# Windowed channel attention with a depthwise convolution: the 128 partitions hold two halves of one image instead of two images

## What is computed

```
xn  = groupnorm(x, 32 groups)                      # two channels to a group, mean and variance over the image
qkv = depthwise3x3(w_qkv @ xn + b_qkv) + b_dw      # 1x1 product to 192 channels, then a 3x3 per channel, zero padding
q, k, v = windows of 8 x 8 pixels, 4 heads of 16 channels
attn = softmax(q k^T * temperature)                # channels x channels (16 x 16) in each window and head
out  = (attn v) * gelu(v w_mlp^T + b_mlp)          # the gate is exact gelu over the 64 pixels of a window
y    = x + w_proj @ out + b_proj
```

## Time and profile before

| | us |
|---|---|
| Median of three runs | 672.14 |
| The profiled execution | 675.23 |
| Its span in the trace | 673.4 |
| PE busy (share of the span) | 623.8 (93%) |
| PE weight loads busy | 547.5 (81%) |
| DVE busy | 504.5 (75%) |
| ACT busy | 481.4 (71%) |
| Mean granted TensorE clock | 0.982 |

### The profile page before, as it was taken

One profiled execution on the slowest core, in us unless ns is written; L12 is line 12 of the kernel. 1 busy time (PEld: TensorE's weight loads), 2 busy tenths in 40 slices (PEclk: granted clock), 3 DMA queues, 4 the chain that ended last, 5 costly groups with the idle time before them and its releaser, 6 DMA issues.

```text
span 673.4 us, 32951 instructions
## 1 busy us (share of the span) xinstructions
PE 623.8 (93%) x15300; PEld 547.5 (81%) x15300; DVE 504.5 (75%) x791; ACT 481.4 (71%) x631; POOL 0.3 (0%) x5
## 2 busy tenths in 40 slices
PE   3888799999999999999999999999999999999975
PEld 2787688888979888888879888898989888898963
DVE  4872588787988788786877678687867778687774
ACT  2642768687777878687787878787787868777743
POOL 0000000000000000000000000000000000000000
PEclk9898899999999999999999999999999999999996
DMA  8872114417071524314060412305050412303023
GB/s 363 267 220 73 34 35 144 150 42 253 22 247 50 183 98 118 113 44 153 4 195 6 135 67 73 130 8 195 4 180 24 136 67 70 127 4 127 4 82 49
DMA packets 29242, 72.32 MB, mean 107 GB/s; under 512 B 9801, under 2 KB 16329, under 8 KB 24233
## 3 DMA queue, kind: packets, MB, share of 16 engines
q1 hardware_dynamic: 28674, 68.57, 31.5%
q10 hardware_dynamic: 432, 1.65, 0.6%
HBM read 53.44 MB, written 16.78 MB: 104 GB/s over the span
## 4 chain that ended last, share of the span: by engine, by line
PE 87%; ACT 5%; DVE 3%; issue 3%; DMA 1%; ACTq 0%; DVEq 0%
PE unit_ps L750 28%; PE unit_ps L715 26%; PE rest_ps L867 10%; PE rest_ps L818 6%; PE rest_ps L844 5%; PE rest_ps L790 5%; PE rest_ps L828 4%; ACT z L337 2%; DMA patches<-in_hot 1%; PE rest_ps L684 1%; ACT dw L337 1%; PE rest_ps L715 1%; PE unit_ps L677 0%; DVE gate L521 0%; DVE scores L531 0%
## 5 line engine op out<-in xcount | busy, mean ns | idle before, releaser
L337 ACT ACTIVATE z<-unit_ps 100x768 f32<-100x768 f32 x244 | 184.7, 808 | 58.3 <-PE unit_ps L715 58.3
L715 PE MATMUL unit_ps<-consts,patches 64*100 64x192 f32 x1984 | 193.7, 335 | 8.6 <-ACT z L337 6.5
L750 PE MATMUL unit_ps<-z,dw 103*64 103x64 f32 (+2 forms) x6144 | 194.3, 224 | 3.2 <-issue 1.9
L750 PEld LDWEIGHTS unit_ps<-z,dw 103*64 103x64 f32 (+2 forms) x6144 | 185.7, 139 | 10.7 <-issue 8.6
L715 PEld LDWEIGHTS unit_ps<-consts,patches 64*100 64x100 f32 x1984 | 152.5, 163 | 25.6 <-ACT z L337 11.1
L337 ACT ACTIVATE qkv<-unit_ps 128x1024 f32<-128x1024 f32 x78 | 79.1, 1014 | 31.7 <-PE unit_ps L750 31.6
L867 PE MATMUL rest_ps<-gate,consts 128*128 128x256 f32 x256 | 74.7, 416 | 3.4 <-DVE gate L521 3.2
L531 DVE TENSOR_TENSOR scores<-rest_ps,consts 128x512 f32<-128x512 f32 x60 | 41.3, 689 | 48.7 <-PE rest_ps L790 48.6
L521 DVE TENSOR_TENSOR gate<-rest_ps,gate 128x512 f32<-128x512 f32 x64 | 44.1, 688 | 44.9 <-PE rest_ps L844 40.7
L358 ACT ACTIVATE v_t<-rest_ps 128x512 f32<-128x512 f32 x64 | 38.2, 596 | 40.9 <-PE rest_ps L828 39.4
L352 ACT ACTIVATE scores<-scores 128x512 f32<-128x512 f32 (+1 forms) x64 | 39.5, 617 | 29.1 <-DVE scores L538 27.5
(11 more groups left out here) (61 smaller groups left out, 533.5 us busy)
## 6 DMA issues: line engine op xcount, KB each, us to landing
staged<-in_x SPq DMA_DIRECT2D x17, 1024.0 KB, 4.9
out_y<-staged SPq DMA_DIRECT2D x15, 1024.0 KB, 5.4
T<-in_x SPq DMA_DIRECT2D x12, 1152.0 KB, 7.0
seen<-in_x SPq DMA_DIRECT2D x32, 256.0 KB, 3.1
qkv<-in_x SPq DMA_DIRECT2D x6, 1024.0 KB, 14.0
T<-in_x SPq DMA_DIRECT2D x3, 1088.0 KB, 6.8
staged<-in_x SPq DMA_DIRECT2D x2, 512.0 KB, 23.2
out_y<-staged SPq DMA_DIRECT2D x4, 256.0 KB, 3.1
```

What stands on the lines that cost most here:

```text
L337: return nc.scalar.activation(to, of, ACT.Copy)
L715: last = nc.tensor.matmul(to[0:NPATCH, t, b * QKV:(b + 1) * QKV], patches[image, b, g], w1[image], start=True, stop=True)
L750: last = nc.tensor.matmul(to[h * HW:(h + 1) * HW, m // 8, m % 8 * NW:(m % 8 + 1) * NW], dw[0:used, c, :], z[0:used, c, :], start=True, sto ...
```

## The change

The partitions become channel c of the upper half (rows 0 to 63) and channel c of the lower half (rows 64 to 127) of one image. A chunk is then one band of 16 rows of each half; an image has four bands, and four images make 16 chunks again. With that:

- Every DMA between the image and the partitions becomes two, one to or from partitions 0 to 63 and one to or from 64 to 127. T takes its neighbour rows from across the middle of the image; the first one comes by a small DMA (`halo_in`).
- The first load is one image (4 MB in 10 DMAs) instead of two. It fits into `qkv`'s space, so `prefill` of chunks 0 and 1 no longer waits for the statistics.
- The group product averages over four partitions instead of two. The mean and variance are made four times instead of twice, three of them inside the run, at chunks 3, 7 and 11.
- 48 slices instead of 32 go through `look`: two to a step in the first eight steps, then one to a step up to step 39.
- The border rows are loaded once. Three rows more take the top rows back where all rows are used, since top and bottom now meet in different halves: K goes from 109 to 112, and `top_rows` goes.
- `idle_products(24)` becomes `idle_products(4)`.
- ACT's queue loads the taps and the build table beside the image as before; those lines stay.

The diff, cut to its core:

```diff
-PAIRS = B // 2
+SIDE = H // 2
-BANDS = H // BAND
-CHUNKS = PAIRS * BANDS
+BANDS = SIDE // BAND
+CHUNKS = B * BANDS
-EDGES = 9
+EDGES = 12
-STATS = H // STAT_ROWS
+STATS = SIDE // STAT_ROWS
-LOOKS = (2, 2, 1, 1)
...
-    return n if n < BANDS else CHUNKS - 1 - n
+    return n % BANDS if n // BANDS % 2 == 0 else BANDS - 1 - n % BANDS
...
-    if (n, a) == (BANDS - 1, 0):
-        fill += [("mean", 1)]
-    if (n, a) == (BANDS - 1, 1):
-        fill += [("var", 1)]
+    if a == 0:
+        fill += [("mean", image) for image in next_image(n)]
+    if a == 1:
+        fill += [("var", image) for image in next_image(n)]
     return fill
+
+
+def next_image(n):
+
+    return [n // BANDS + 1] if n % BANDS == BANDS - 1 and n + 1 < CHUNKS else []
...
-    return min(i // BATCHES * sum(LOOKS) + sum(LOOKS[:i % BATCHES]), STATS)
+    early = 2 * BATCHES
+    return min(2 * i if i < early else STATS + i - early, (B - 1) * STATS)
...
-        first = [loaded[:, n * BAND:(n + 1) * BAND] for n in range(6)] + [staged[:, n] for n in range(2)]
+        first = [loaded[:, n * BAND:(n + 1) * BAND] for n in range(BANDS)]
...
+        sides = [slice(t * C, (t + 1) * C) for t in range(2)]
...
             def load_t(n):
                 sp.wait_ge(patches_ready, n)
-                lo, hi, to = band_rows(n)
-                sp.dma_start(T[:, to:to + hi - lo, 1:1 + W], halves[n // BANDS, :, lo:hi, :]).then_inc(t_in, 16)
+                for t in range(2):
+                    lo, hi, to = halo_rows(n, t)
+                    sp.dma_start(T[sides[t], to:to + hi - lo, 1:1 + W], x[n // BANDS, :, lo:hi, :]).then_inc(t_in, 16)
...
-                if n < 2:
-                    sp.wait_ge(seen_done, 2 * BANDS)
-                else:
-                    sp.wait_ge(stored[n % 2], (n // 2) * 16)
...
+                if n >= 2:
+                    sp.wait_ge(stored[n % 2], (n // 2) * 32)
+                for t in range(2):
+                    sp.dma_start(staged[sides[t], n % 2],
+                                 x[n // BANDS, :, chunk_rows(n, t), :]).then_inc(staged_in[n % 2], 16)
...
-            def top_rows(which, p):
-                wait_full(sp, ("dw", which * BANDS, 5))
...
+            def load_first(n, rows, done):
+                for t in range(2):
+                    top = t * SIDE + n * BAND
+                    sp.dma_start(first[n][sides[t], rows],
+                                 x[0, :, top + rows.start:top + rows.stop, :]).then_inc(done, 16)
...
+            sp.dma_start(T[sides[1], 0, 1:1 + W], x[0, :, SIDE - 1, :]).then_inc(halo_in, 16)
+            sp.wait_ge(x_last, 32)
+            sp.dma_start(z[NPATCH:K].rearrange("p c w -> p (c w)"), edges).then_inc(edges_in, 16)
...
                 if band == 0:
-                    pad(T[:, 0:1, :], pair)
+                    pad(T[sides[0], 0:1, :], pair, sides[0])
...
-                nc.vector.bn_stats(stats[:, p], seen[:, p % 2]).then_inc(seen_done, 1)
+                nc.vector.bn_stats(stats[:, p % STATS], seen[:, p % 2]).then_inc(seen_done, 1)
...
-            idle_products(24)
+            idle_products(4)
...
-                                           -bottom, bottom and left, bottom and right)
+                                           -bottom, bottom and left, bottom and right,
+                                           top, -(top and left), -(top and right))
...
-    group = (0.5 * (chan[:, None] // 2 == chan[None, :] // 2)).astype(f)
+    group = (0.25 * (chan[:, None] % C // 2 == chan[None, :] % C // 2)).astype(f)
```

More of the change, by code:

```diff
@@ L212, in build @@
         number = units()
-        halves = x.rearrange("(j b) c h w -> j (b c) h w", j=PAIRS)
-        bands = out.rearrange("(j b) c h w -> j (b c) h w", j=PAIRS)
         def wait_full(engine, unit):
@@ L272, in prefill @@
-                rows = slice(band_of(n) * BAND, (band_of(n) + 1) * BAND)
-                sp.dma_start(staged[:, n % 2], halves[n // BANDS, :, rows, :]).then_inc(staged_in[n % 2], 16)
-            def load_seen(i):
-                for p in range(looks_until(i), looks_until(i + 1)):
-                    if p >= 2:
-                        sp.wait_ge(seen_done, 2 * BANDS + p - 1)
-                    rows = slice(p * STAT_ROWS, (p + 1) * STAT_ROWS)
-                    sp.dma_start(seen[:, p % 2], halves[1, :, rows, :]).then_inc(seen_in[p % 2], 16)
@@ L404, in _ @@
                     v_up(i)
-                if (n, a) == (BANDS - 1, 2):
-                    deviation(1)
+                if a == 2:
+                    for image in next_image(n):
+                        deviation(image)
                 now = gelus_in(i)
@@ L472, in normaliser, with pad @@
                 link(nc.vector.tensor_tensor(norm[:, pair, 1:2], small[:, 4:5], small[:, 5:6], ALU.mult))
-            def pad(edge, pair):
+            def pad(edge, pair, rows=slice(0, P)):
                 size = edge.shape[1] * edge.shape[2]
-                over = zeros[:, 0:size] if size <= 2 * (BAND + 2) else zeros[:, 0:1].to_broadcast([P, size])
+                over = zeros[rows, 0:size] if size <= 2 * (BAND + 2) else zeros[rows, 0:1].to_broadcast(
+                    [rows.stop - rows.start, size])
                 over = over.rearrange("p (r c) -> p r c", r=edge.shape[1])
-                link(nc.vector.tensor_scalar(edge, over, norm[:, pair, 0:1], None, ALU.add))
+                link(nc.vector.tensor_scalar(edge, over, norm[rows, pair, 0:1], None, ALU.add))
             def pads(n):
@@ L639, in _ @@
                     look(p)
-                if looks_until(i) < STATS <= looks_until(i + 1):
-                    aggregate(1)
+                if a == BATCHES - 1:
+                    for image in next_image(n + 1):
+                        aggregate(image)
             scores_up(TAIL)
@@ L743, in depthwise @@
                 if v == 0:
-                    pe.wait_ge(edges_in, 16 * (1 + PIECES * sum(n >= m for m in (BANDS - 1, CHUNKS - 1))))
+                    pe.wait_ge(edges_in, 16)
                 used = rows_used(n)
```

86 lines of the change are left out of this document (46 added, 40 removed).

## The result

The changed kernel takes 692.96 us (median of 4, 685.65 to 695.64) beside 671.67 of the kernel before in the same comparison: ratio 1.0284, 95% interval 1.0191 to 1.0377, so about 20 us slower. The forecast was 674.6, its range ended at 681.5. The profiled execution took 695.64, the longest of the four; its span is 693.8. Times are medians and ratios are of means, which leave out the executions that took over 1.5% more than the kernel's shortest (two of e11_warm24, one of e8_t_halves_only).

The account below looks back on a forecast made before the run. The prediction took PE, 87% of the chain, to bound the kernel. Head -2.0, steady part +4.1 and tail +0.4 gave +2.5: 677.7 us against the profiled execution, 674.6 against the median, range 667 to 681.5.

Parts of the forecast that it names:

- Head, by the build: Head up to the first channel product: build table lands at 15.7, first channel product at 35.8 instead of 37.83; -2.0 us.
- rival 1: All transfers: both halves together reach the full 419 GB/s; head -6.3, total 670.3, or 667 without PE's stop; chance 0.23.
- Head, behind the image: Head after the image: T of chunk 1 lands at 47.7 to 50.4, costing PE 0 us at 230 GB/s.
- Rival 2: Depthwise units: PE's instructions come late behind slower half transfers; two more stops cost +6.8, giving 681.4; chance 0.17.
- rival 3: First channel products: with 20 fewer warming products PE starts cold at 1.2 GHz, costing 1.5 to 3 us; chance 0.08.
- Steady part: Steady chunks: two more image changes cost +2.8 and slices in third batches +1.3; together +4.1 us.
- Tail: End of the run: each last store becomes two, one more DMA issue on the path; +0.4 us (bounds 0 and 1).

Follow-up runs that it names:

- e11_warm24: The changed kernel with 24 warming products ahead of the statistics, as before, instead of 4: 681.59 us, ratio 1.0119.
- e8_t_halves_only: The changed kernel with partitions ordered 2c + t and single 128-partition transfers for all but T, which stays in halves; nothing left out: 678.46 us, ratio 1.0077.
- e1_joined: The changed kernel with each pair of 64-partition transfers made one over 128 partitions; output not the reference's: 671.58 us, ratio 0.9996.
- e7_t_first: The changed kernel with T of chunk 1 issued ahead of the second staged block, not behind it: 687.86 us, ratio 1.0213.
- e13_short20: The changed kernel with 20 more products, of one column each, ahead of the statistics: 679.48 us, ratio 1.0145.
- e14_long_same_count: The changed kernel with 9 products of 512 columns ahead of the statistics and 1 behind, replacing 4 and 6 of 192: 694.38 us, ratio 1.0308.
- e17_before_warm4: The kernel before with 4 warming products ahead of the statistics instead of 24, all transfers over 128 partitions: 672.03 us, ratio 1.0016.
- e5_no_change: e1_joined without the work of the image changes, all images normalised with image 0's numbers; output not the reference's: 662.95 us, ratio 0.9845.
- e4_two_queues: The changed kernel with upper halves' transfers on SP's queue and lower halves' on POOL's, each with its own semaphores: 686.15 us, ratio 1.0218.
- e15_joined_short20: e1_joined with 20 more products of one column ahead of the statistics: 675.91 us, ratio 1.0045.

## Why the prediction was wrong

1. **Head, by the build (-2.0).** The number held (-2.05), the way to it did not, so that is luck. The table was to land at 15.7 and set the head; it landed at 12.00, so the image beside it gave way, not the table. The weights were ready at 24.65, nearly as before, and the mean product waited for the image: the statistics were done at 29.87, where the sum had 27.5. The mean product came 1.8 us earlier than in the sum (29.93 for 31.7), and from there to the first channel product it took 1.8 us longer (5.85 for 4.08), most of it at the lower clock. The rate chosen, 230 GB/s, is near the 271 and 234 of the first two windows of 8.2 us; which of two transfers it would hold up was wrong. At 420 GB/s e1_joined shows -7.08, for which rival 1 had -6.3. (At 250 GB/s, an estimate in the prediction, the same steps give a sum of +1.7, where it has +1.9.)
2. **Head, behind the image (0).** This step failed. T of chunk 1 was to land between 47.7 and 50.4; it was there at 53.00. The image was in at 27.86, not 25.2, and the transfers behind it took 25.1 us, where the sum had 22.5 to 25.2. PE's hold was put at 0, and at 2.5 at most; the stop was 2.61. Moved ahead of one staged block (e7_t_first), T came in time and PE's stop behind DVE went, but one of 2.58 us without a releaser stood in its place, so T's lateness alone is not shown to cost the 2.61.
3. **Rival 2, late instructions (0.17).** This was the case, and the sum had it at nothing: the step that failed by most. Its mark, waits named "issue" in the depthwise units, is there: 3.48 us at 62.22, with no packet of instructions beside 1.16 MB of T. The argument against it was that steady chunks move 132 GB/s and show no such stop. That holds for the program and the transfers of before, not for others: there are three such stops, in turn 5, step 17 and step 29, and the trace of e13_short20, with 40 more records, has none of them. The changed kernel and e1_joined run the same 15,268 records of PE in the same order, so their starts can be set side by side. Of the 8.4 us that the middle stage of the changed kernel is longer, some 6 come at five places where PE's instructions are late (1.8, 0.5, 0.9, 1.3 and 1.8 us at 128.79, 137.24, 206.37, 255.32 and 372.79), and 1.3 between 84.1 and 90.8, where the granted clock is 0.50. The rule of the Trainium skill, "Runtime: NRT & Kernel Launch", section "Instruction fetch mechanics", that the queue mostly hides the fetch, holds for most places in every kernel here; it failed once by 1.91 us in the kernel before, and by 3.48, 1.58, 0.96, 1.51 and 1.75 us here.
4. **The step that was missing.** "The head has 20 products less" was weighed as a cold start (rival 3) and, under rival 1, as a chance to lose a stop. That it could also bring stops was not. Given half transfers, the same kernel takes 692.96, 686.50 or 679.48 us with 0, 10 or 20 small products more (their intervals touch; those of the changed kernel and of e11_warm24 do not). With 128 partitions it makes no difference in the steady part.
5. **Rival 3, a cold start (0.08).** Not the cause of the 20 us: e14_long_same_count is busy nearly as long ahead of the mean product as e11_warm24 (7.99 us, 9.75) and no faster than the changed kernel, and e17_before_warm4 loses nothing. But it was there, since PE waited for the statistics: 1.3 us ahead of the first channel product (2.61 for 1.35), where rival 3 had 1.5 to 3. The lower clock cost more behind the long stops: 2.6 us in the first depthwise units and 1.3 in the channel unit after them.
6. **Steady part (+4.1).** Right for the work that it names: e1_joined takes 4.3 us more than before in the middle stage, and a change is worth 1.5 where 1.40 were taken. Plain chunks without a stop still repeat after 38.0. The changed kernel lost 12.76 there; the rest is point 3.
7. **Tail (+0.4).** 2.8, and 1.5 in e1_joined. PE has a stop of 1.75 us at 675.58, as in e1_joined (2.31 at 650.34), named "issue" in both, that before doesn't have there. It too belongs to the place of the instructions: e5_no_change lacks it.

Of the 24.3 us between the spans of the changed kernel and e1_joined, 5.0 are the image's, 9.5 those of points 2 and 3 before the first scores, 8.4 come in the middle stage, 1.3 in the tail. The first comes with the halves alone, 1.3 of it by the clock; the rest needs the halves and the place of the instructions together, since either without the other lacks most of it (e1_joined; e13_short20, whose span is 6.6 us longer than e1_joined's, all of it in its first channel product, 6.72 later).

Why a fetch beside a half transfer stops PE at one place and not at another, the traces answer in part. PE's instructions come in packets of 16 KB by queue q8, 120 packets for the 30,834 instructions of PE in the trace, so one for every 256 or so:

```profile
q8 instruction: 120, 1.97, 1.2%
```

Counted by 256 from PE's first instruction, the stops without a releaser lie at the same place in each block, the 194th or 195th, in all twenty traces. That goes for every one of over 0.65 us behind 38 us, but for the 1.4 us ahead of one channel unit, which all kernels have, and one of 0.88 in e4_two_queues. The packet for the next block starts when PE has entered the one before it, 0.60 us later in the median of the kernel before and 0.95 in the changed kernel. At the stops at 62.22, 128.79, 255.32 and 372.79 it started 6.20, 4.90, 4.96 and 5.56 us later, behind data of q1, and PE went on 1.4 to 1.5 us after it had ended. A delay of 6.40 us from 431.71 on stopped nothing, since PE had work for 9.0 us in that block; depthwise records use one up in 3.8 (128 of the 192 in 5.75). So a stop takes a long transfer under way as PE enters a block (in the steady part only kernels with half transfers show such stops), and quick work in that block. Products added upstream move the work against the blocks, and a later start moves both against the transfers. Open is in which order the DMA engines serve the two queues, how much of the delay comes from T's small packets, and why executions of one kernel differ by 10 us.

## What to carry to other kernels

Splitting one transfer of 128 partitions into two of 64 takes a third off the rate here, and a second queue does not give it back: choose the layout by the stride that lets one transfer reach all partitions (half t of channel c at partition 2c + t did, at 64t + c didn't). A slower bulk transfer can be paid twice, by who waits for its data and by TensorE's instructions behind it; the second price moves with what is added or removed upstream, so test a change that shifts TensorE's program at more than one instruction count before it is judged. A long stop of TensorE costs more than its length: behind those of 2.61 and 3.48 us the granted clock was lower, and 2.6 us went there. Behind the three of up to 1.58 us in the steady part it stayed at 1.00 (90.9 to 667.6).

## What the runs showed of the hardware

- Two half transfers on two queues moved 272 GB/s where two on one queue moved 271 and one of 128 partitions 420, the engines being busy all the time in each (1.01 to 1.03).
- The same half transfers stop TensorE or not with the number of its instructions and with its start: in the traces 3.48 us at 62.22 with 4 warming products, 0.59 us at most in these units with 20 short ones more, none without a releaser with as many instructions and a start 2.2 us later (e14_long_same_count).
- TensorE's instructions came in packets of 16 KB, one for 256, each started when the block before was entered (0.60 us later in the median of the kernel before). In the changed kernel the long stops ended 1.4 to 1.5 us after the end of a packet that had started 4.90 to 6.20 us late.
- A product of one column is not small: 20 of them, with weights of 128 columns, and the lower clock that came with them (0.50 between 28.6 and 38.7) made the first channel product 6.10 us later (e15_joined_short20).
